# One-core language-model block with a mixture-of-experts layer: loads held behind a gather, expert outputs in single pieces, reordered drain, filler matmuls

## The reference, cut to what matters

```python
x = emb[tokens] * sqrt(256) + pos                    # 16 x 256 tokens, 256 wide
p = softmax(q(x) @ k(x).T / 16, axis=1);  h = p @ v(x)
u = layernorm(h)                                     # then a state-space block (SSD, chunks of 128)
zxbcdt = layernorm(u) @ in_proj.T                    # 1288 columns: z 512, conv 768, dt 8
y = ssd(silu(conv4(xBC)), softplus(dt)) ; y = rms(y * silu(z)) ; h = h + u + y @ out_proj.T
v2 = layernorm(h)                                    # router: 8 experts, top 2, capacity 1024 rows each
xb = rows of v2 scattered to (expert, slot);  y_e = gelu(xb @ w1[e]) @ w2[e]   # 256 -> 1024 -> 256
out = h + scatter_add(weight * y_e) + bias
```

## Time and profile before

| what | us |
|---|---|
| median of 3 runs | 958.42 (957.29 to 958.7) |
| the profiled execution, its own time | 958.16 |
| its span, first to last instruction | 956.4 |
| PE busy | 887.6 (93%) |
| DVE busy | 631.6 (66%) |
| ACT busy | 529.1 (55%) |
| POOL busy | 505.9 (53%) |
| mean granted TensorE clock | 0.965 of full |

### The profile page before, as it was taken

How to read it: one execution, slowest core, us unless ns; L and a number is a source line. 1 busy time by engine, 2 the same in 40 slices (tenths; PEclk the granted TensorE clock), 3 DMA queues, 4 the chain that set the end, 5 groups by cost and what they waited for, 6 DMA issues and landing times.

```text
span 956.4 us, 17255 instructions
## 1 busy us (share of the span) xinstructions
PE 887.6 (93%) x5580; PEld 785.6 (82%) x5580; DVE 631.6 (66%) x1662; ACT 529.1 (55%) x1094; POOL 505.9 (53%) x503
## 2 busy tenths in 40 slices
PE   5799999999999999999998539999999999999994
PEld 3688888888888888888886429999999999999993
DVE  2477899888988898889887344646363636363631
ACT  1466776677667767776766134545444544444430
POOL 6257776787678767877788311232333232323342
PEclk8799999999999999999998759999999999999998
DMA  8900011001000000000000034343343433332120
GB/s 269 330 26 12 34 46 33 22 33 33 12 22 13 23 13 23 20 16 14 21 22 26 14 103 132 90 88 105 67 109 72 109 72 104 72 105 28 23 61 34
DMA packets 48653, 58.62 MB, mean 61 GB/s; under 512 B 6336, under 2 KB 43819, under 8 KB 48624
## 3 DMA queue, kind: packets, MB, share of 16 engines
q1 hardware_dynamic: 33552, 41.05, 13.1%
q0 software_dynamic: 13632, 17.02, 10.6%
q10 hardware_dynamic: 1440, 0.17, 0.1%
HBM read 34.14 MB, written 29.75 MB: 67 GB/s over the span
## 4 chain that ended last, share of the span: by engine, by line
PE 81%; DVE 10%; issue 3%; POOL 2%; DMA 2%; ACT 1%; DVEq 0%; POOLq 0%; SPq 0%
PE bank L1592 13%; PE bank L1593 13%; PE bank L1594 13%; PE bank L1387 11%; PE bank L1497 5%; PE bank L1332 4%; PE bank L1477 4%; PE bank L1371 3%; PE bank L1346 3%; PE bank L1362 3%; PE bank L1353 3%; PE bank L1449 2%; DVE seg L1051 2%; PE bank L1512 2%; PE bank L1604 2%
## 5 line engine op out<-in xcount | busy, mean ns | idle before, releaser
L637 POOL DMA_INDIRECT out<-ye,tok_slot x56 | 96.7, 1727 | 254.3 <-DMA out<-ye,tok_slot 138.0
L877 ACT ACTIVATE hf<-bank 128x512 f32<-128x512 f32 x128 | 79.5, 621 | 202.4 <-PE bank L1594 201.1
L1264 DVE TENSOR_TENSOR h_lo<-hf,h_hi 128x512 fp32r<-128x512 f32 x128 | 88.6, 693 | 99.9 <-ACT h_hi L879 99.9
L1592 PE MATMUL bank<-w_hi,h_hi 128*128 128x256 f32 x512 | 146.2, 286 | 0.0
L1593 PE MATMUL bank<-w_lo,h_hi 128*128 128x256 f32 x512 | 144.9, 283 | 0.0
L1594 PE MATMUL bank<-w_hi,h_lo 128*128 128x256 f32 x512 | 144.9, 283 | 0.0
L1023 DVE SCALAR_TENSOR_TENSOR xc<-bank,cw,xc 128x253 f32<-128x253 f32 (+2 forms) x288 | 128.2, 469 | 1.7
L1592 PE MATMUL bank<-xe_hi,w_hi 128*128 128x512 f32 x256 | 100.8, 394 | 2.7 <-DVE xe_lo L1256 2.7
L1593 PE MATMUL bank<-xe_lo,w_hi 128*128 128x512 f32 x256 | 100.4, 392 | 0.0
L1594 PE MATMUL bank<-xe_hi,w_lo 128*128 128x512 f32 x256 | 100.2, 391 | 0.0
L585 POOL DMA_INDIRECT slots_dram<-rows,slot x64 | 63.4, 991 | 67.8 <-DVE slot L1152 53.2
(11 more groups left out here) (203 smaller groups left out, 2311.2 us busy)
## 6 DMA issues: line engine op xcount, KB each, us to landing
w_raw<-w SPq DMA_DIRECT2D x16, 1024.0 KB
slots_dram<-zero_row SPq DMA_DIRECT2D x1, 8320.0 KB, 29.7
xe<-slots_dram SPq DMA_DIRECT2D x16, 520.0 KB, 4.4
out<-hb SPq DMA_DIRECT2D x16, 256.0 KB, 2.1
w_raw<-in_wT SPq DMA_DIRECT2D x1, 1288.0 KB, 9.1
slots_dram<-rows,slot POOLq DMA_INDIRECT x64
out<-ye,tok_slot POOLq DMA_INDIRECT x64, 3.7
xg<-emb,idx POOLq DMA_INDIRECT x36, 4.1
```

The lines of the kernel that those rows point to most:

```text
L637: g.indirect_dma_start(out, bass.IndirectOffsetOnAxis(ap=tok_slot[q][:, j:j + 1], axis=0), ye[q][:, j, :], None, compute_op=ALU.add).then_ ...
L877: sc.activation(hf[m % 2][:, :], h_bank[i % H_BANKS][:, :], ACT.Gelu_apprx_tanh)\
L1264: vc.tensor_tensor(h_lo[:, m, :], hf[m % 2][:, :], h_hi[:, m, :].bitcast(F32), ALU.subtract)\
L1592: te.matmul(out_, hi, rhi, start=first_, stop=False)
```

## The change

1. **Loads behind the first gather.** SP's `w_in` and `w_out`, and all ten small loads of ACT, wait for `gathered[0]` (both gathers of batch 0).
2. **The last turn written out.** The loop runs turns 2 to 7; turn 8 is called with `final=True`, so POOL issues no gathers that nobody uses, and its second half has no `to_xT` and no `embedded`. In that half POOL's second `segment_inputs` moves ahead of `free_rows`, `with_bias` and `second_root`.
3. **Roots ahead of the drain's scatters.** In the half with `b` and no `f`, `gated_root` and `second_root` stand before the four scatters.
4. **First slots in two pieces.** The first 512 rows of expert 0 come by two DMAs, and PE starts to turn the first two pieces when the first has landed.
5. **Expert outputs in pieces.** Each piece of 128 rows has a count of its own in `y_psum` and `ye_ready`, alternates between two banks, and is weighed alone. Of the last expert, pieces 0 to 3 are added as the others are; only pieces 4 to 7 are fetched, summed on DVE and written.
6. **Fillers.** `keep_clock` multiplies `ident` with itself into a bank that is free. They stand on PE in places where it waits: 7 and 2 at the start, 36 in the first half, 2 to 4 at some ten places of the first draining half, 28 in the last, 32 before the wait for `part_done`, 10 (of 32 rows) after it and 9 before the first product.

```diff
+    half(0, Turn(turns), Turn(turns - 1), Turn(turns - 1), Turn(turns), True)
+    half(1, Turn(turns), Turn(turns), Turn(turns - 1), None, True)
     half(0, None, Turn(turns), Turn(turns), None)
     half(1, None, None, Turn(turns), None)
...
+        FILL = {'t': 3, 'scores': 2, 'attend': 5, 'hT': 18, 'dt': 8}
+        DRAIN = {'state': 2, 'seg0': 3, 'seg1': 4, 'v2T': 4, 'seg2': 2, 'seg3': 2, 'own': 2, 'yT0': 2, 'yT1': 2, 'out': 1}
+        LAST = {'v2T': 20, 'route': 2, 'choices': 6}
...
+            sp.wait_ge(gathered[0], gathered.per_turn)
             sp.dma_start(w_in[:, :, :], in_wT.rearrange("(k p) n -> p k n", p=P)).then_inc(s_win, 16)
...
+            act.wait_ge(gathered[0], gathered.per_turn)
             for dst, src in small:
                 act.dma_start(dst, src).then_inc(s_small, 16)
             act.wait_ge(s_wqk, 1)
...
             def write_sums():
-                for j in range(JS):
-                    hold(pool, ye_ready, 2 + (NE - 1) * (JS // 2) + (j // 2 + 1 if j < JS // 2 else j + 1 - JS // 4))
+                for j in range(JS // 2):
+                    add_rows(NE, 1, j)
+                for j in range(JS // 2, JS):
+                    hold(pool, ye_ready, 2 + JS * (NE - 1) + j + 1)
...
                 def weigh(g):
...
+                    for n in range(4):
+                        if half == NG - 1 and n >= 2 and not (last and q):
+                            low_weights(r * 2 + q, 1 - q, n - 2, (w1_split, w2_split)[n - 2])
...
+            def keep_clock(spare, times):
+                for _ in range(times):
+                    te.matmul(bank[spare][1][:, 0:P], ident[:, :], ident[:, :], start=True, stop=True)
...
+            keep_clock(1, 2)
             to_xT(Turn(1), 0)
             pe.wait_ge(s_wqk, 2)
...
+            keep_clock(0, 32)
             pe.wait_ge(part_done, 1)
```

More of the change, by code:

```diff
@@ L604, in half @@
                     skip_x(b, q, 1)
-                if f:
+                if f and not final:
                     gather_next(f, p)
@@ L608, in half @@
                     describe_rows(t, p)
+                if b and not f:
+                    gated_root(b, q)
+                    second_root(b, q)
+                if t:
                     scatter_rows(t, p)
-                if b:
+                if b and f:
                     gated_root(b, q)
@@ L613, in half @@
                     segment_inputs(f, p, 0)
+                if f and not nf:
+                    segment_inputs(f, p, 1)
                 if t:
@@ L1304, in experts @@
                         split_x(g + 1)
-                    if last and g >= NG:
-                        weigh_onto(g)
-                    else:
-                        weigh(g)
+                    weigh(g)
                     if g + 1 == NG:
@@ L1528, in half @@
                 q = 1 - p
+                filling, draining = not b and not t, not f
+                if filling:
+                    keep_clock(q, FILL["t"])
                 if f:
@@ L1549, in half @@
                     x_to_rows(b, q, 1)
+                if b and draining:
+                    keep_clock(p, DRAIN["seg2"])
+                if b:
                     segment_sums(b, q, 2)
+                if draining and not b:
+                    keep_clock(p, LAST["route"])
                 if t:
                     route(t, p)
+                if b and draining:
+                    keep_clock(p, DRAIN["seg3"])
                 if b:
@@ L1555, in half @@
                     chunk_state(b, q)
+                if b and draining:
+                    keep_clock(p, DRAIN["own"])
+                if b:
                     own_chunk(b, q, 0)
+                if filling:
+                    keep_clock(q, FILL["hT"])
                 if f:
@@ L1560, in half @@
                     from_state(b, q)
+                if draining and not b:
+                    keep_clock(p, LAST["choices"])
                 if t:
                     choices_before(t, p)
+                if b and draining:
+                    keep_clock(p, DRAIN["own"])
                 if b:
                     own_chunk(b, q, 1)
+                if b and draining:
+                    keep_clock(p, DRAIN["yT0"])
+                if b:
                     to_yT(b, q, 0)
+                if filling:
+                    keep_clock(q, FILL["dt"])
                 if f:
@@ L1574, in half @@
                     project_channels(f, p, 1)
+                if b and draining:
+                    keep_clock(p, DRAIN["yT1"])
                 if b:
@@ L1586, in _ @@
             run_batches(te.Fori, half, PAIRS)
+            keep_clock(0, 32)
             pe.wait_ge(part_done, 1)
             pe.sem_inc(y_psum, Y0)
+            for _ in range(10):
+                te.matmul(bank[0][1][:, 0:P], ident[0:32, :], ident[0:32, :], start=True, stop=True)
             def three(out_, hi, lo, rhi, rlo, first_, last_):
@@ L1656, in experts @@
                         turn_x(g + 1)
-                    if last and g + 1 == 2 * NG:
-                        last_product(g)
-                    else:
-                        second_product(g)
+                    second_product(g)
             experts(1, None)
```

139 lines of the change are left out of this document (73 added, 66 removed).

## The result

The change is faster by 0.3%: 956.32 us (median of seven, 954.65 to 957.87) against 958.68 (957.29 to 960.47) for the kernel before on the same chip, ratio 0.9969, 95% interval 0.9957 to 0.9982. I had forecast 948.8. The sign was right; three quarters of the gain did not come. The profiled execution took 954.65 itself, the quickest of the seven, with a span of 952.7 against 956.4.

The account below looks back on a forecast made before the run. PE bounds the experts (busy 570 to 940 us), so only seams could gain: start +1.0, drain -2.7, experts' start -2.8, tail -5.1, sum -9.6, giving 948.6 profiled and 948.8 median. The range was 943.5 to 954.5.

Parts of the forecast that it names:

- Start, +1.0: Start: later first product +3.7, waits kept at full clock by fillers -2.7, so +1.0 us in all.
- the +3.7: Start: `wqk` copied behind ACT's ten issues, first product ends at 21.8 instead of 18.0; +3.8, of which 3.7 kept.
- Last turn, -0.4: Last turn: one `to_xT` and one `embedded` fewer on PE and DVE, -0.4 us.
- Drain, -2.3 behind `msq`: Drain: roots first and full clock bring the last scatters earlier; -2.7 including last turn's 0.4, with 1.3 charged for clock.
- First product, -1.1 behind the scatters: Experts' start: first two pieces land 0.7 us before the whole half and their turn is faster, -1.1 us.
- the turn of 8 pieces takes 0.9: Experts' start: turning eight pieces takes 0.9 us, not 1.97 less its tail; part of the -1.1.
- each takes 0.44: Rival that the clock never rises at the seams: each filler takes 0.44 us; chance 0.04 slower, 0.03 no change.
- Clock of the first products, -1.7: Experts' start: first matmuls run at full instead of half clock from 568 to 572 us, -1.7 us.
- Tail, -5.1: Tail after PE's last matmul: with outputs in pieces the last write lands at 946.5 instead of 951.7, -5.1 us.
- By pieces that start is 888.3: Tail: adds of the expert before start at 888.3 instead of 892.40, and the four end at 908.
- The tail's adds are slower: 951.7: Rival: gather not quicker or tail's adds slower, +2.8 or +3 us, giving 951.7; chance 0.15.
- 969: Rival: clock never rises at the seams, 20.8 us in all, giving 969; chance 0.04 slower, 0.03 no change.

Follow-up runs that it names:

- small: The change with ACT's ten small loads at the start of its list again, only SP's two big loads behind the first gather: 952.00 us, ratio 0.9933.
- pairs: The change with the expert outputs in pairs again, eight fetches and eight writes at the end: 958.09 us, ratio 0.9981 to the kernel before.
- s_free: small, with the drain not waiting for its four scatters to land before the last bias row and description of rows: 952.27 us, ratio 0.9915.
- s_entry: small, with 46 instead of 32 fillers before `part_done`, ten of 128 rows instead of 32, four instead of nine behind the turn: 949.62 us, ratio 0.9887.
- piecesonly: The kernel before with only the expert outputs in pieces (four adds, four fetches, four writes at the end): 955.00 us against 959.46, ratio 0.9955.
- b_adds2: Kernel of combined corrections, drain's scatter wait kept, with two last pieces added and six fetched and written instead of four and four: 943.51 us against 943.76.
- again: The change unaltered, run again for a second trace: 957.11 us against 959.40 for the kernel before, ratio 0.9975.
- after: The change itself in its first profiled execution: 954.65 us, span 952.7, against a span of 956.4 for the kernel before.
- s_roots: small, with the drain's four scatters ahead of the roots again as in the kernel before: 954.27 us, ratio 0.9939.
- s_seg: small, with `second_root` ahead of the second `seg` pair again in the last full half: 950.41 us, ratio 0.9897.

## Why the prediction was wrong

- **Start, +1.0: right.** +0.17 and +1.30. The gather took 3.8 as forecast, the ten issues held ACT as forecast. The product took 2.58 and 3.62 (I had 3.75), as the clock rose during it or only at its end. What I left unsaid is that the +3.7 was avoidable; small wins it back.
- **Last turn, -0.4: about right**, -0.76 and -0.64 between the first two rows of the table.
- **Drain, -2.3 behind `msq`: half of it in one trace, an eighth in the other.** The distance from `msq` to the last scatters was 43.73, and is 42.50 and 43.44 (45.72 in pairs). The direct steps came: `nm` 3.6 later, `h` right behind PE. The output product took 3.69; I had put down 3.5, where twice the 1.89 of the earlier trace rows is 3.78. Short were two things. `hb` and the description of the rows stand behind the landing of the four scatters on POOL, which I had put at 548.2 and which ended at 550.5; and the stretch at half clock behind `nm`, charged with 1.3, was not the same from trace to trace.
- **First product, -1.1 behind the scatters: failed.** +0.18 and +1.15. The step that failed is "the turn of 8 pieces takes 0.9": the 32 fillers before it ended 2.8 us too early, the ten of 32 rows behind that wait did not bring the clock back, and at 0.50 the turn took 1.97 and nine fillers 3.69, more than the 2.65 that they were to fill. Where fillers reached up to POOL's release, the turn took 1.35 (s_free) and 1.30 (s_entry). I had named this ("each takes 0.44") only for the case that the clock never rises.
- **Clock of the first products, -1.7: right**, -2.16 in both traces, of which 0.55 belong to the pieces, as piecesonly has them alone.
- **Tail, -5.1: failed, the main error.** It was put together from durations that were nearly right (adds 4.7, a write 3.24) and a start that was not. "By pieces that start is 888.3", 4.1 earlier, took PE's piece for the event; but DVE was still in `xe_hi` and `xe_lo` until 885.4 and weighed the piece then. With the seams ahead in it the forecast's first add is 883.8 and its last write 939.5, and they came at 886.70 and 945.75: of the 6.25, 2.9 are this start (0.7 of them from the seams ahead), 1.1 the fetch (7.5, not 6.4), 1.9 the gaps of the writes, where the one late landing is, 0.4 the eight adds. And I never asked what one piece costs POOL's queue in either form: an add 4.6 to 4.8, with one of 5.7 in four; a fetch and a write 1.28 + 3.24 = 4.5. That sum says at once that four adds in place of four fetches and writes win nothing, and b_adds2 shows it. A small slip besides: the times of the paragraph (949.27 to 944.0) give 5.3, the sum took 5.1.
- **The rivals.** "The tail's adds are slower: 951.7" pointed at the right place with too small a price. The clock did rise; nothing decided for 969 (its own terms give 969.6). The range ended at 954.5, 1.8 us below the median, since no case took the tail's whole 5.1 away.
- **One trace for seven runs.** The seams of this kernel move by 1 to 3 us between executions, and the profiled one was the quickest of seven. Against `again` the account is: start to last weigh -0.6 instead of -4.5, tail 0 instead of -5.1.

## What to carry to other kernels

Where an engine's queue of DMAs ends the kernel, price each form of a step by how long it holds the queue, landing included, and look for who really releases the first entry; an earlier first entry can move the end, while trading one form of a step for another that holds the queue as long does not. Before a group of loads is held behind an event, ask for each load what stands behind it in its own queue: here two large loads were worth 3.8 us behind the gather, and ten small ones cost 5.1. Read more than one trace of a program before a difference of a few us is put down to an edit. Fillers pay while they end before what they wait for and keep the clock up to it; the same fillers at half clock last twice as long and delay the work that they were put there to speed up.

## What the hardware showed that I had not expected

- **Tiny DVE rows last as long as POOL's large ones.** `lm` and `lv`, 128x2 on DVE, take 1.97 and 1.94 us beside the 1.89 us `seg` rows of POOL, where they took 0.17 and 1.27 before; `topf`, 128x4, takes 1.83 beside `hb` and 0.17 without it. In again, the same program as after, `lm` took 0.17: it began 0.05 us before POOL's next `seg` row (514.70 and 514.75), where in after it was 0.04 (513.46 and 513.50), so a few hundredths of a us decide whether the row stretches. `gm`, which reads PSUM, takes its 0.41 beside `hb`. The Trainium skill (SBUF — State Buffer, SBUF: two separate sides) says that VectorE in a two-port mode and GpSimd lock the shared pair of ports for a whole instruction and the loser waits. The lengths of the rows fit this; in which mode these rows ran, no run here shows. So a row moved on POOL also sets how long its neighbours on DVE take.
- **One instruction packet of 16 KB on a DMA engine goes with a landing that is 0.9 to 2.2 us late**, in seven writes of 88, read from the order of times as told above.
- **The level of the clock in one seam is not fixed by the program.** Up to the last full half, small, s_roots, s_entry, s_seg and s_free have the same instructions, and behind the same wait (4.2 to 5.4 us) the granted clock from 32 to 36 us was 1.00, 0.70, 0.65, 0.50 and 0.50. The waits of small and s_seg were 4.19 and 4.18 us, and their clocks 1.00 and 0.50. In the drain, behind the wait for `nm`, it was 0.86, 0.83, 0.67 and 1.00 in after, again, pairs and small, in the stretch from 10 to 20 us behind `msq`. PE had the same list there in each.
